# Attention over image blocks: four diagonal squares of the first transferred group copied on chip, group results moved to the head of ScalarE's slot, and a shift column made from one operand

## The reference

```python
y = group_norm(x, 4 groups) * gn_gamma + gn_beta           # per image
q, k, v = split(w_qkv @ y + b_qkv)                          # each 128 x 1024
scores = q.T @ k * 128 ** -0.5                              # 1024 x 1024
a = softmax(scores, axis=-1) @ v.T
out = x + (w_out @ a.T + b_out)
```

## Time and profile before

| | us |
|---|---|
| median of 3 runs | 141.91 |
| lowest and highest of the runs | 140.3, 143.17 |
| profiled execution | 141.43 |
| its span | 139.6 |

### The profile page before, as it was taken

The page is one execution under the profiler, slowest core; times in us unless marked ns, Lnnn a source line. Parts: engine busy times, 40 slices in busy tenths (PEclk is TensorE's granted clock), DMA queues, the critical chain, the costliest instruction groups (busy, mean ns, idle before and its releaser), DMA issues.

```text
span 139.6 us, 1850 instructions
## 1 busy us (share of the span) xinstructions
PE 131.1 (94%) x573; PEld 90.6 (65%) x573; DVE 99.0 (71%) x189; ACT 69.8 (50%) x126; POOL 68.5 (49%) x75
## 2 busy tenths in 40 slices
PE   7999999999999949999989999999799999899991
PEld 7987677777776625676555656776455576554691
DVE  0489687999999996787786986698866826751211
ACT  3154768775774365644652276575723355850000
POOL 6032165697338647944095667933583345113000
PEclk9999999999999999999999999999999999999999
DMA  4940000000069679980997349963997179812031
GB/s 138 340 198 0 0 5 0 2 0 0 0 134 207 147 155 208 207 228 8 208 204 156 107 97 203 208 170 77 209 204 188 34 168 211 200 68 75 0 113 38
DMA packets 7065, 17.16 MB, mean 123 GB/s; under 512 B 1936, under 2 KB 2192, under 8 KB 7056
## 3 DMA queue, kind: packets, MB, share of 16 engines
q1 hardware_dynamic: 6768, 16.78, 49.3%
q10 hardware_dynamic: 288, 0.27, 0.6%
HBM read 2.36 MB, written 2.10 MB: 32 GB/s over the span
## 4 chain that ended last, share of the span: by engine, by line
PE 72%; DVE 12%; SPq 7%; ACT 3%; issue 2%; DMA 2%; DVEq 0%; ACTq 0%
PE mixed L791 28%; SPq L239 7%; PE scores L747 7%; PE scores L748 7%; PE scores L750 7%; DVE scores L551 6%; PE scores L817 4%; DVE crossed L575 3%; PE turned L764 3%; PE turned L694 3%; ACT probs L388 2%; PE mixed L694 2%; DMA crossed<-crossed 2%; DVE crossed L562 1%; ACT result L408 1%
## 5 line engine op out<-in xcount | busy, mean ns | idle before, releaser
L310 POOL TENSOR_SCALAR probs<-probs,inv_sum 128x1024 f32<-128x1024 f32 x32 | 36.0, 1126 | 48.1 <-DVE inv_sum L556 48.1
L551 DVE TENSOR_SCALAR_CACHE_REDUCE scores<-scores,key_bias 128x1024 f32<-128x1024 f32 x31 | 40.0, 1290 | 14.6 <-PE scores L750 14.4
L388 ACT ACTIVATE probs<-scores,neg_max 128x1024 f32<-128x1024 f32 x32 | 35.7, 1116 | 23.5 <-DVE scores L551 22.7
L791 PE MATMUL mixed<-crossed,v 128*128 128x512 f32 x96 | 44.7, 593 | 2.0 <-DMA crossed<-crossed 2.0
L747 PE MATMUL scores<-y_hi,z_hi 128*128 128x512 f32 x62 | 34.8, 561 | 0.0
L575 DVE STREAM_TRANSPOSE crossed<-probs 128x1024 f32<-128x1024 f32 x24 | 29.7, 1239 | 0.0
L791 PEld LDWEIGHTS mixed<-crossed,v 128*128 128x128 f32 x96 | 17.3, 190 | 16.2 <-issue 15.4
L748 PE MATMUL scores<-y_lo,z_hi 128*128 128x512 f32 x62 | 24.4, 394 | 0.0
L750 PE MATMUL scores<-y_hi,z_lo 128*128 128x512 f32 x62 | 19.2, 391 | 0.0
L747 PEld LDWEIGHTS scores<-y_hi,z_hi 128*128 128x128 f32 x62 | 11.7, 189 | 7.8 <-issue 6.2
L748 PEld LDWEIGHTS scores<-y_lo,z_hi 128*128 128x128 f32 x62 | 11.7, 189 | 7.2 <-issue 5.7
(11 more groups left out here) (148 smaller groups left out, 159.5 us busy)
## 6 DMA issues: line engine op xcount, KB each, us to landing
crossed<-crossed SPq DMA_DIRECT2D x96, 128.0 KB, 2.3
out_dram<-result SPq DMA_DIRECT2D x7, 256.0 KB, 2.5
xs<-in_x_dram SPq DMA_DIRECT2D x2, 512.0 KB, 6.4
xs<-in_x_dram SPq DMA_DIRECT2D x3, 256.0 KB, 5.1
xs<-in_x_dram ACTq DMA_DIRECT2D x1, 256.0 KB, 3.6
ws<-in_weights_dram SPq DMA_DIRECT2D x1, 256.0 KB, 4.0
out_dram<-result SPq DMA_DIRECT2D x2, 128.0 KB, 1.9
vecs<-in_vectors_dram ACTq DMA_DIRECT2D x1, 3.0 KB, 4.2
```

The lines of the kernel that those rows point to most:

```text
L310: pool.tensor_scalar(probs[:, i % RING, :], probs[:, i % RING, :], inv_sum[:, i:i + 1], 1.0, ALU.mult, ALU.mult).then_inc(s_probs, 1)
L388: act.activation(probs[:, i % RING, :], scores[:, i % 2, :], ACT.Exp, bias=neg_max[:, i:i + 1], scale=-1.0, accum_out=row_sum[:, i:i + 1]) ...
L551: dve.tensor_scalar(scores[:, i % 2, :], scores[:, i % 2, :], key_bias[:, b % 2, i:i + 1], None, ALU.subtract, ALU.min, accum_out=neg_max[ ...
L791: mm = pe.matmul(bank, v[:, b % 2, k, :], at, start=first, stop=final)
```

## The change

1. `swap(1)` issues 12 transfers, k = 1, 2, 3. The four diagonal squares of group 1 are copied within their partitions, 32 x 1024 elements each: squares 0 and 1 by ScalarE at the end of slots 8 and 9, squares 2 and 3 by GpSimd in slots 8 and 10, after that slot's `normalise` (and in slot 8 after rstd). TensorE waits for all four before the first tile of group 1, and DVE before the flip of block 12, which writes over their source.
2. `biased_result` stands at the head of ScalarE's slot, ahead of the copies and of the exponential, where it stood behind them.
3. `norm_b` is made by `tensor_scalar` with two column operands in place of `scalar_tensor_tensor` with two tensor inputs.

```diff
-    SWAP = 16 * SQ * SQ
+    DIAGONAL_SLOTS = {"scalar": {8: 0, 9: 1}, "gpsimd": {8: 2, 10: 3}}
...
+        s_diagonal = {"scalar": sem("diagonal_by_scalar_copied"), "gpsimd": sem("diagonal_by_gpsimd_copied")}
...
-            return SWAP * len([g for g in SWAPPED if g <= group and g % 2 == group % 2])
+            return sum(16 * (SQ * SQ - (SQ if g == 1 else 0)) for g in SWAPPED if g <= group and g % 2 == group % 2)
+
+        def diagonal_square(of, g):
+            return crossed[32 * g:32 * g + 32, of, g * N:(g + 1) * N]
...
-                for k in range(SQ):
+                for k in range(1 if group == 1 else 0, SQ):
...
+                    if BLOCKS * b + i in DIAGONAL_SLOTS["gpsimd"]:
+                        g = DIAGONAL_SLOTS["gpsimd"][BLOCKS * b + i]
+                        pool.wait_ge(s_flipped, QB)
+                        pool.wait_ge(s_probs, BLOCKS * b + i + 3)
+                        pool.wait_ge(s_rstd, 3)
+                        pool.tensor_copy(diagonal_square(HOME[1], g), diagonal_square(3, g)).then_inc(s_diagonal["gpsimd"], 1)
+                        pool.wait_ge(s_diagonal["gpsimd"], len([n for n in DIAGONAL_SLOTS["gpsimd"] if n <= BLOCKS * b + i]))
...
+                    if i % QB == 3 and BLOCKS * b + i >= 11:
+                        biased_result((BLOCKS * b + i - 11) // QB)
                     if not swapped(BLOCKS * b + i):
                         turned_copy(BLOCKS * b + i)
...
                         exponentials(*after(b, i, 2))
-                    if i % QB == 3 and BLOCKS * b + i >= 11:
-                        biased_result((BLOCKS * b + i - 11) // QB)
                     if i == (1 if b == 0 else 2) and not last:
                         y_head(b + 1)
+                    if BLOCKS * b + i in DIAGONAL_SLOTS["scalar"]:
+                        g = DIAGONAL_SLOTS["scalar"][BLOCKS * b + i]
+                        act.wait_ge(s_flipped, QB)
+                        act.activation(diagonal_square(HOME[1], g), diagonal_square(3, g),
+                                       ACT.Copy).then_inc(s_diagonal["scalar"], 1)
...
-                    dve.scalar_tensor_tensor(out=norm_b[:, b:b + 1], in0=minus_means[:, b - lo:b - lo + 1],
-                                             scalar=norm_a[:, b:b + 1], in1=BETA, op0=ALU.mult,
-                                             op1=ALU.add).then_inc(s_norm, 1)
+                    dve.tensor_scalar(norm_b[:, b:b + 1], minus_means[:, b - lo:b - lo + 1], norm_a[:, b:b + 1], BETA,
+                                      ALU.mult, ALU.add).then_inc(s_norm, 1)
...
+                if n == 3 * QB:
+                    dve.wait_ge(s_diagonal["scalar"], 2)
+                    dve.wait_ge(s_diagonal["gpsimd"], 2)
...
+                        if group == 1:
+                            pe.wait_ge(s_diagonal["scalar"], 2)
+                            pe.wait_ge(s_diagonal["gpsimd"], 2)
```

## The result

The changed kernel takes 142.23 us (median of 21 executions) against 141.26 us (21 of the kernel before). The ratio is 1.0116, 95% interval 1.0092 to 1.0140: **1.2% slower**, where 141.1 us, a third of a microsecond faster, was forecast. The medians are of all executions, 0.97 us apart; the ratio leaves out those more than 1.5% above the fastest of their kernel, and comes to about 1.6 us.

What follows compares the result with a forecast made beforehand. TensorE, busy 94% of the span, was taken as the bound, losing 2.2 us ahead of group 1 and 0.95 us in slots 16 and 24 each. 1.55 - 1.9 = -0.35 us from 141.43 gave 141.1 us, range 139.3 to 143.4.

Steps and rivals of the forecast that it cites:

- The sum: Whole kernel: restart 1.55 us later, results at the head 1.9 us gained, together -0.35 us, so 141.1 us.
- rival (c): Six products behind TensorE's pause ahead of group 1 run at 1.2 GHz, taking twice as long: +2.6, 143.7 us; chance 0.06.
- The second copy as the step that decides: GpSimd's slot 10 copy, behind normalising block 12, releases TensorE for group 1 at 53.15 us, against 51.59 before.
- Rival (b): GpSimd's diagonal copies in slots 8 and 10 take 2.6 us each; restart 56.1, +2.6, 144.0 us; chance 0.07.
- The results at the head: Slots 16 and 24: value products no longer wait for ScalarE's result, gain 2 x 0.95 = 1.9 us.
- DVE's wait ahead of flip 12: DVE's new wait for the copies before flipping block 12 costs nothing; it had reached that flip only at 53.31.
- The shift column: norm_b from one operand takes 0.22 us instead of 1.03 while GpSimd normalises, so DVE is 0.8 us earlier.
- rival (a): The shift column stays at 1.03 us, restart at 53.9, +0.4 us in sum, 141.8 us; chance 0.2.
- The twelve transfers: Group 1's transfers land by 47.8 or 48.9, before 49.40; by them alone the whole 2.2 us pause would go.
- (d): The last copy comes in time and TensorE goes on with group 1 at 49.4: -4.1, 137.3 us; chance 0.1.
- (e): Moving the results does nothing, something else of ScalarE's slot holds the bank: +1.55, 143.0 us; chance 0.07.

Runs made afterwards that it cites:

- e8_long_pause: The kernel before, with TensorE also waiting ahead of group 1 for the normalising of block 12: 143.68 us, ratio 1.021.
- e7_last_copy_first: The changed kernel with GpSimd copying square 3 before it normalises block 12 in slot 10: 138.42 us, ratio 0.986 to the kernel before.
- e5_early_copies: The changed kernel with square 2 copied ahead of normalising block 9 in slot 7, square 3 in slot 8: 137.08 us, ratio 0.977 to the kernel before.
- e1_heads_only: The kernel before with only biased_result moved to the head of ScalarE's slot: 138.99 us, ratio 0.987.
- e3_column_only: The kernel before with only norm_b made by tensor_scalar: 141.15 us, ratio 1.000.
- e2_copies_only: The kernel before with only the twelve transfers and four copies (biased_result behind the exponential, norm_b by scalar_tensor_tensor): 144.23 us, ratio 1.027.

## Why the prediction was wrong

**The step that failed is the clock.** The sum, 1.55 - 1.9 = -0.35 us, took the products behind the pause at their old pace; the fall of the clock stood beside it as rival (c), with a chance of 0.06, on the ground that no row showed the lower level. It came in 20 of 21 executions. With the term, 1.5 (pause 3.55 against 2.04) + 1.4 (4.21 against 2.81) - 1.9 = +1.0 us; measured +0.97 by the medians and +0.8 by the traces behind the reciprocal of block 11. The ratio gives 1.6 us, which the two kinds of executions of the kernel before can account for. The rival's price was too high. It doubled all six products, but the lower level ended before they did, and the cost is half of the time for which TensorE works at that level. In the changed kernel that was from 55.57 to about 58.4, 2.8 us, and cost 1.4 us; in `e8_long_pause` it was from 53.0 to 56.4, 3.4 us, and cost 1.7 (4.21 and 4.51 for 2.81 us), not 2.6. Whole executions with and without the fall differ by less, 1.2 us in `e8_long_pause` and 1.0 in the changed kernel; why, is not shown. What I should have read: a pause of 3.7 us, forecast in the same sentence, lay outside anything that the trace of before could vouch for; that it showed 1.00 through 2.04 us was no evidence on it. The Trainium skill (TensorE: Matmul & The Clock Gate, Why this matters for your kernels) warns of just such gaps, and I gave the rule less weight than the absence of a row. By that rule these runs agree: in the two kernels whose traces show a pause of 3.5 us, the mean clock was 0.988 or less in 26 of 27 executions.

**The second copy as the step that decides: right.** Forecast: restart at 53.15; measured 55.57 - 2.46 = 53.11. The copies began at 46.28 and 51.93 (forecast 46.2 and 51.9), took 1.03 us (1.12), and GpSimd's wait for its own result 0.17. `e7_last_copy_first` and `e5_early_copies` show it by moving that copy alone, or both. Rival (b) falls.

**The results at the head: right,** with the size: -1.9 forecast, -1.8 alone, -2.0 on top of the early copies.

**DVE's wait ahead of flip 12** was put at nothing because DVE had reached that flip only at 53.31. With DVE 0.8 us ahead it did wait, 0.46 us for the last copy, but TensorE did not pay: from its restart to the end the changed kernel takes 87.33 us, less 1.40 for the clock 85.93, as in `e1_heads_only`.

**The shift column: right in kind.** 0.27 in place of 0.22 us; rival (a) falls with `e3_column_only`. The Trainium skill (SBUF — State Buffer, Who interferes with whom) counts the one-source form from SBUF to SBUF among those that can take the shared ports, if its operands meet certain conditions; for one element a partition these traces show no hold: 0.27 us, begun 0.10 us into GpSimd's normalising, in slot 9 of `e3_column_only` and in slot 17 of the changed kernel. In the changed kernel the 1.03 us would not have come back either, as `e2_copies_only` shows: there the column's order against GpSimd had changed.

**The twelve transfers: right, and hidden.** They had landed when TensorE asked; `e5_early_copies` restarts without any wait. The 2.2 us that they can give were there and were held up by one copy.

**Rivals (d) and (e) fall** for this kernel; (d) is what `e5_early_copies` makes of it, at 137.1 us, where 137.3 was worked out.

## What to carry to other kernels

When a wait on the busiest engine is split into parts, each part must be due before the old one was: look where the last of them stands in its own engine's queue, and put it before the long work, not behind it. When a change lengthens a pause of TensorE, price the products behind it at the lower clock level as well, even if the trace shows only the higher one, since a trace can say nothing about pauses longer than its own. And a pause that can't be removed can be filled: 14 products of zeros were worth about 1.6 us.

## What the hardware showed that was not expected

The fall of the clock is not the same in each execution. With a pause of 3.16 us in the trace it came in 4 of 6 executions of one kernel, with 3.5 us in 26 of 27 of two. In the kernel before the mean clock was 0.988 in 3 of 29 executions, with 142.9 us in place of the median's 141.19, and 0.985 and 0.988 in 2 of 15 on the other chip; whether these falls belong to the pause of 2 us no trace shows. The fall can come before the engine works again (near 55.0 for a restart at 55.57), with its first product (`e2_copies_only`, 52.5 for 52.48) or 0.9 us after it (53.0 for 52.10), and in all three traces it lasts 3.4 us.

The first products of an execution can be slow for other lengths too: in the profiled execution of the changed kernel the start cost 2.46 us more. The clock rows show 1.00 there, but that is no reading. The recorded clock begins, at 1.00, only at 14.0 us in this trace and at 6.5 us in the trace of before; for the time ahead of it there is no record, and the table then shows 1.00. The products say more. The first line is of the changed kernel, the second of the kernel before, at the same place in the program; the last two are of the changed kernel, on either side of 14.0 us:

```profile
6.68 0.77 PE L838 MATMUL scores<-blank 128*128 128x128 f32 x2
...
6.58 0.47 PE L817 MATMUL scores<-blank 128*128 128x128 f32 x2
...
13.62 0.58 PE L878 MATMUL scores<-y_lo,z_hi 128*128 128x512 f32 x1
14.04 0.40 PE L880 MATMUL scores<-y_hi,z_hi 128*128 128x512 f32 x1
```

In the nine traces that have the record, the later it begins the later the first reciprocal of a row sum comes: 15.9 to 16.0 us where it begins at 3.9 to 5.3, 16.5 and 16.6 where it begins at 6.5 and 6.7, and 19.0 where it begins at 14.0. So the slow start looks like the lower level lasting longer, though no row shows that level there; why it lasted until 14.0 us here stays open.
